# An eight-layer transformer on one core: later projections, transposes inside expert blocks, other score banks, and ternary weights prepared in an earlier stage

## The reference

```python
def act_quant(x):
    scale = 127.0 / jnp.clip(jnp.max(jnp.abs(x), axis=-1, keepdims=True), 1e-05)
    return jnp.clip(jnp.round(x * scale), -128, 127) / scale
def weight_quant(w):
    scale = 1.0 / jnp.clip(jnp.mean(jnp.abs(w)), 1e-05)
    return jnp.clip(jnp.round(w * scale), -1, 1) / scale
def bit_linear(x, w):
    return jnp.einsum('bsd,hd->bsh', act_quant(x), weight_quant(w))
h = bit_linear(x, w1)                            # 256 -> 1024
h = depthwise_conv1d(h.transpose(0, 2, 1), conv_w, conv_b)   # 3 taps
return bit_linear(silu(h.transpose(0, 2, 1)), w2)             # 1024 -> 256
```

## Time and profile before

| | us |
|---|---|
| median of 3 runs | 3054.76 (3051.03 to 3055.73) |
| the profiled execution's own time | 3083.54 |
| its span | 3081.8, mean granted PE clock 0.928 |

### The profile page before, as it was taken

The page is one execution under the profiler, slowest core; times in us unless marked ns, Lnnn a source line. Parts: engine busy times, 40 slices in busy tenths (PEclk is TensorE's granted clock), DMA queues, the critical chain, the costliest instruction groups (busy, mean ns, idle before and its releaser), DMA issues. The chain is left out here.

```text
span 3081.8 us, 47764 instructions
## 1 busy us (share of the span) xinstructions
PE 2581.3 (84%) x15928; PEld 1781.0 (58%) x15928; DVE 1374.2 (45%) x4831; ACT 1121.8 (36%) x2609; POOL 824.1 (27%) x878
## 2 busy tenths in 40 slices
PE   6998859999938878979999999984999559999586
PEld 4776437777714434547766555663888436666344
DVE  6987502222133444336643333430111357777665
ACT  4554311111118970114444333331333126666321
POOL 3443030000042210007754344503000401212442
PEclk8999879999979998979999999997999769999798
DMA  4232362222022110034210000035777410000000
GB/s 134 84 116 78 146 204 85 84 86 74 14 95 78 60 42 24 0 93 144 111 45 7 11 6 6 1 123 195 293 285 289 140 34 11 10 8 6 28 7 18
DMA packets 69923, 252.33 MB, mean 82 GB/s; under 512 B 16395, under 2 KB 32040, under 8 KB 52264
## 3 DMA queue, kind: packets, MB, share of 16 engines
...
...
## 5 line engine op out<-in xcount | busy, mean ns | idle before, releaser
L2597 PE MATMUL L_ffne_up<-L_ffne_xT,L_ffne_wu 128*128 128x128 f32 (+1 forms) x2144 | 391.5, 340 | 33.2 <-DVE L_ffne_xT L2521 23.3
L2597 PEld LDWEIGHTS L_ffne_up<-L_ffne_xT,L_ffne_wu 128*128 128x128 f32 x2144 | 332.2, 194 | 92.9 <-ACT L_ffne_hT L2508 27.5
L1349 PEld LDWEIGHTS L_xattn_pt<-ident,L_xattn_p 112*125 112x125 f32 x1536 | 207.3, 189 | 183.4 <-issue 77.5
L1044 POOL TENSOR_SCALAR L_xattn_p<-L_xattn_p,L_xattn_rec 112x375 f32<-112x375 f32 x256 | 311.6, 1225 | 0.0
L1349 PE MATMUL L_xattn_pt<-ident,L_xattn_p 112*125 112x112 f32 x1536 | 257.7, 289 | 20.9 <-DVE L_xattn_pt L1203 16.0
L1203 DVE COPY L_xattn_pt<-L_xattn_pt 125x336 f32<-125x336 f32 x448 | 216.9, 499 | 125.6 <-PE L_xattn_pt L1349 125.5
L2583 PE MATMUL L_ffne_dn<-L_ffne_wd,L_ffne_hT 128*112 128x256 f32 (+1 forms) x1200 | 266.2, 379 | 1.5 <-issue 1.5
L1186 DVE TENSOR_REDUCE L_xattn_least<-L_xattn_s 112x1 f32<-112x375 f32 x256 | 128.4, 543 | 250.7 <-PE L_xattn_s L1337 250.5
L2583 PEld LDWEIGHTS L_ffne_dn<-L_ffne_wd,L_ffne_hT 128*112 128x112 f32 (+1 forms) x1200 | 216.9, 183 | 39.7 <-issue 2.1
...
L1127 ACT ACTIVATE L_xattn_p<-L_xattn_ssb,L_xattn_least 112x375 f32<-112x375 f32 x256 | 153.8, 602 | 129.9 <-DVE L_xattn_least L1192 129.0
L1127 ACT ACTIVATE L_xattn_p<-L_xattn_s,L_xattn_least 112x375 f32<-112x375 f32 x256 | 145.1, 569 | 140.7 <-DVE L_xattn_least L1186 140.6
...
## 6 DMA issues: line engine op xcount, KB each, us to landing
...
```

Of the source, the lines that this page charges most:

```text
L1044: p = pool.tensor_scalar(p_sb[:, head % RP, :], p_sb[:, head % RP, :], rec[:, h, head:head + 1], None, ALU.mult)
L1349: m = pe.transpose(pt_ps[head % 2][0:KP, 0, kt * S:(kt + 1) * S], p_sb[:, head % RP, kt * KP:(kt + 1) * KP], ident[0:S, 0:S])
L2597: m = pe.matmul(up_ps[s % RING][k][:, 0, 0:RH], wu[:, h, c, k * FF + f * 128:k * FF + (f + 1) * 128], xT[:, h, c, q * RH:(q + 1) * RH], st ...
```

## The change

Six of the twelve stages are touched.

- Tanh attention: the projection of a batch and its residual come one batch later, the projection between the second and the third chunk of scores. PE's and DVE's loops are written out for all 16 batches.
- Both expert stages: the transposes of the next block's rows, and the copies, are placed after given up-steps (after steps 6, 8, 10, 12, 14, or after step 4) and no longer at the block's end.
- Wide attention: the four free banks are three for scores and one for jobs up to turn 6, and two and two from turn 7 on; the jobs have other slots there; transposes of a pair stand together ahead of the jobs, and both jobs ahead of the products. The narrow attention keeps its order and banks.
- Second routing stage: the ternary layer's weights are loaded here, ahead of the fills, and DVE makes the ternary weights (q1, q2), the 24 taps and a bf16 identity behind the slots. PE sums the weight sums ahead of the last four hosted projections. These tiles are kept until the end.
- Ternary layer: no weights are prepared; DVE normalises and spreads the first four batches; POOL normalises from the fifth on.

```diff
-                    if not isinstance(b, int) or b < NB - 1:
+                    if b < NB - 1:
...
-                    if not isinstance(b, int) or b > 0:
-                        ch = Chain(dve, chain, (b - 1) * PER)
+                    ch = Chain(dve, chain, max(0, (b - 2) * PER + 1))
+                    if b > 1:
+                        residual(b - 2, h, ch)
+                    if b > 0:
                         take_o(b - 1, 1 - h)
                         divide(b - 1, ch)
-                        residual(b - 1, 1 - h, ch)
...
-                each_batch(dve, body)
-                ch = Chain(dve, chain, (NB - 1) * PER)
+                for b in range(NB):
+                    body(b, b % 2)
+                ch = Chain(dve, chain, (NB - 2) * PER + 1)
+                residual(NB - 2, 0, ch)
                 take_o(NB - 1, 1)
...
                         transpose_x(b + 1, 1 - h)
+                    if b > 1:
+                        project(b - 2)
                     scores(b, h, 2)
...
-                    if not first:
-                        project(b - 1)
...
-                each_batch(pe, body)
+                for b in range(NB):
+                    body(b, b % 2)
+                project(NB - 2)
...
-        slots = [[K[0]], [K[1]], [K[2]], [K[3]], [K[4]], [K[5]], [K[6]], [K[7]], [Q[0]], [Q[1], V[0]],
-                 [Y], [V[1], V[2]], [V[3]], [V[4]], [V[5]], [X]]
+        slots = [[K[0]], [K[1]], [K[2]], [K[3]], [K[4]], [K[5], K[6]], [K[7]], [], [Q[0]], [Q[1]], [Y],
+                 [V[0]], [V[1], V[2]], [V[3]], [V[4], V[5]], [X]]
+        slots_loaded = [[], [], [], [], [], [], [], [], [Q[0]], [Q[1]], [Y], [], [], [], [], [X]]
...
-    NS, NJ = (3, 1) if wide else (4, 1)
...
+    FREE = 4 if wide else 5
+    SWITCH = FROM - 1 if wide else NB
...
+    def score_banks(b):
+
+        return 2 if wide and b >= SWITCH else FREE - 1
...
+        def jobs_at(b, head):
+
+            return (slots_loaded if wide and b < SWITCH else slots)[head]
+
         def slot_jobs(run, b, h, head, kinds):
-            for kind, i in slots[head]:
+            for kind, i in (jobs_at(b, head) if wide else slots[head]):
...
+            first = 2 if wide and turn >= SWITCH else FREE - 1
+            spare = range(first, FREE)
+            at = spare[planned[first] % len(spare)]
+            planned[first] += 1
+            bank_of[kind, i, b] = at
+            if at in last_user:
+                bank_free[kind, i, b] = last_user[at]
+            elif at < FREE - 1:
+                bank_free[kind, i, b] = ("score", SWITCH * H - 1, 0)
+            last_user[at] = (kind, b, i)
...
+        def wait_bank(pe, kind, i, b):
+
+            if (kind, i, b) in bank_free:
+                was, of, n = bank_free[kind, i, b]
+                if was == "score":
+                    pe.wait_ge(exp_done, of + 1)
+                else:
+                    pe.wait_ge(done[was], made(was, of, n))
...
-                    after(pe, exp_done if wide else low_done, b * H + pair + 2 - NS)
+                    after(pe, exp_done if wide else low_done, b * H + pair + 2 - score_banks(b))
...
                         scores(b, h, pair)
+                        together = wide and b >= SWITCH
                         trail(b, h, pair, LT, turn_p)
+                        if together:
+                            trail(b, h, pair + 1, LT, turn_p)
                         slot_jobs(job, b, h, pair, "kqvxyz")
-                        trail(b, h, pair + 1, LT, turn_p)
+                        if together:
+                            slot_jobs(job, b, h, pair + 1, "kqvxyz")
+                        else:
+                            trail(b, h, pair + 1, LT, turn_p)
                         if (pair - LP) % SIDE == 0:
                             trail(b, h, pair, LP, products)
-                        slot_jobs(job, b, h, pair + 1, "kqvxyz")
+                        if not together:
+                            slot_jobs(job, b, h, pair + 1, "kqvxyz")
...
+class TernaryWeights:
...
+    def begin(self, sp, ins):
+        for to, src in ((self.w1[:, :], ins["L3_ffn_w1"]), (self.w2[:, :], ins["L3_ffn_w2"]),
+                        (self.cw[:, :, :], ins["L3_ffn_conv_w"]), (self.cb[:, :], ins["L3_ffn_conv_b"])):
+            sp.dma_start(to, src).then_inc(self.w_in, 16)
...
+    def sum(self, pe, bank):
+        pe.wait_ge(self.ones_done, 1)
+        pe.wait_ge(self.wsum_done, 1)
+        pe.matmul(bank[:, 0, 0:2], self.ones[:, :], self.wsum[:, :], start=True, stop=True).then_inc(self.wsum_out, 1)
+
+    def prepare(self, dve, bank):
+
+        c = Chain(dve, self.chain)
+        c.step(dve.tensor_copy(self.identb[:, :], self.core.ident[:, :]))
+        dve.wait_ge(self.w_in, 64)
+        for n, w in enumerate((self.w1, self.w2)):
+            r = dve.tensor_reduce(self.wsum[:, n:n + 1], w[:, :], AX.X, ALU.add, apply_absolute_value=True)
+        r.then_inc(self.wsum_done, 1)
+        dve.wait_ge(self.wsum_out, 1)
+        c.link(dve.tensor_scalar(self.wmean[:, :], bank[:, 0, 0:2], 1.0 / (D * FF), EPS, ALU.mult, ALU.max))
+        c.link(dve.reciprocal(self.wscale[:, :], self.wmean[:, :]))
+        c.step(dve.tensor_scalar(self.cws[:, :, :], self.cw[:, :, :], self.wmean[:, 0:1], None, ALU.mult))
+        for n, (w, q) in enumerate(((self.w1, self.q1), (self.w2, self.q2))):
+            c.link(dve.tensor_scalar(w[:, :], w[:, :], self.wscale[:, n:n + 1], 1.0, ALU.mult, ALU.min))
+            c.link(dve.tensor_scalar(w[:, :], w[:, :], -1.0, self.MAGIC, ALU.max, ALU.add))
+            c.step(dve.tensor_scalar(q[:, :, :].rearrange("p a b -> p (a b)"), w[:, :], self.MAGIC, None, ALU.subtract))
+        for f in range(FC):
+            for j in range(3):
+                c.step(dve.tensor_scalar(self.taps[:, f, j, :], self.core.ident[:, :], self.cws[:, f, j:j + 1], None, ALU.mult))
+        dve.wait_ge(c.sem, c.n)
...
             def _(sp):
-                for to, src in ((w1[:, :], ins["L3_ffn_w1"]), (cw[:, :, :], ins["L3_ffn_conv_w"]),
-                                (cb[:, :], ins["L3_ffn_conv_b"]), (w2[:, :], ins["L3_ffn_w2"])):
-                    sp.dma_start(to, src).then_inc(w_in, 16)
...
-                for b in range(GB):
-                    normalize(b)
-                for b in range(GB):
-                    spread(b)
+                pool.wait_ge(xn_done, GB)
                 for b in range(GB, 2 * GB):
                     normalize(b)
-                pool.wait_ge(w_in, 64)
-                pool.wait_ge(wmean_done, 1)
-                ch.link(pool.tensor_scalar(w2[:, :], w2[:, :], wscale[:, 1:2], 1.0, ALU.mult, ALU.min))
-                ch.link(pool.tensor_scalar(w2[:, :], w2[:, :], -1.0, MAGIC, ALU.max, ALU.add))
-                pool.tensor_scalar(q2[:, :, :].rearrange("p a b -> p (a b)"), w2[:, :], MAGIC, None,
-                                   ALU.subtract).then_inc(q2_done, 1)
...
-                for f in range(FC):
-                    for j in range(3):
-                        r = act.activation(taps[:, f, j, :], ident[:, :], ACT.Copy, scale=cws[:, f, j:j + 1])
-                    r.then_inc(taps_done, 1)
-                    if f == 0:
-                        for b in range(GB):
-                            take_inverse(b)
+                for b in range(GB):
+                    take_inverse(b)
...
-                dve.wait_ge(w_in, 64)
-                for n, w in enumerate((w1, w2)):
-                    r = dve.tensor_reduce(wsum[:, n:n + 1], w[:, :], AX.X, ALU.add, apply_absolute_value=True)
-                r.then_inc(wsum_done, 1)
+                dve.wait_ge(rstd_done, 1)
+                for b in range(GB):
+                    dve.tensor_scalar(xn[:, b, :], x[:, b, :], core.mv[:, b, 0:1], core.rstd[:, b:b + 1],
+                                      ALU.subtract, ALU.mult).then_inc(xn_done, 1)
...
                 largest(0)
-                dve.wait_ge(identb_done, 1)
-                dve.wait_ge(wsum_out, 1)
-                c.link(dve.tensor_scalar(wmean[:, :], sc_ps[:, 0, 0:2], 1.0 / (D * FF), EPS, ALU.mult, ALU.max))
-                c.link(dve.reciprocal(wscale[:, :], wmean[:, :]))
-                dve.tensor_scalar(cws[:, :, :], cw[:, :, :], wmean[:, 0:1], None, ALU.mult).then_inc(wmean_done, 1)
-                c.link(dve.tensor_scalar(w1[:, :], w1[:, :], wscale[:, 0:1], 1.0, ALU.mult, ALU.min))
+                for b in range(GB):
+                    dve.tensor_scalar(invw[:, b, :], ones[0:S, :], amax[:, b:b + 1], None, ALU.mult).then_inc(invw_done, 1)
                 quantize(0)
-                c.link(dve.tensor_scalar(w1[:, :], w1[:, :], -1.0, MAGIC, ALU.max, ALU.add))
                 quantize(1)
-                dve.tensor_scalar(q1[:, :, :].rearrange("p a b -> p (a b)"), w1[:, :], MAGIC, None,
-                                  ALU.subtract).then_inc(q1_done, 1)
                 take_turned(0)
...
                 keys.begin(sp, ins)
+                if tw:
```

(20 more changed lines are left out.)

168 lines of the change are left out of this document (80 added, 88 removed).

## The result

The changed kernel takes 2952.87 us (median of 4 runs, 2949.59 to 2957.65) against 3052.9 of before (4 runs). The ratio is 0.9674 with a 95% interval of 0.9656 to 0.9692: 99.5 us off, where 61 were forecast and the range ended at 2967. Its profiled execution took 2949.59 us (span 2947.9, mean granted clock 0.934).

What follows compares the result with a forecast made beforehand. Each touched stage was taken to have its own limit: ACT and PE in tanh, PE in attentions and experts, POOL's puts in routing, waits in ternary. Terms -13 -10 -7 -20 +11 -23 = -62 gave 2993 us, range 2967 to 3021.

Steps and rivals of the forecast that it cites:

- Part 2: First expert stage, 8 blocks: PE's waits at the block's end go, 10 us off, bounds 7 and 11.
- part 4: Second expert stage, 35 blocks: the border wait for the xT copy goes, 20 us off, bounds 10 and 23.
- rival of late rows: Expert stages: next block's rows land after their mid-block use, making the kernel slower, up to 3097 us; chance 0.02.
- Part 3: Wide attention: job waits -12, exposed loads -5, score waits +8 and +2; sum -7, bounds +2 and -18.
- exposed loads: Wide attention: loads exposed between a K job and the scores are hidden by the new order, -5, possible 0 to 10.
- Part 1: Tanh attention: ACT's 0.98 us wait at each of 15 batch borders goes, 13 us off, bounds 5 and 15.
- The unrolled bodies: Tanh attention: writing out the loops was taken as 0, with 3 us either way left inside the bounds.
- Part 5: Second routing stage: 3.6 us from the delayed context load plus 7 from slowed puts, +11, bounds 0 and 18.
- Part 6: Ternary stage: opening 11.4 us earlier, group 0 stall and half-clock convolution gone; 23 us off, bounds 17 and 25.
- Pieces don't follow: Rival, whole kernel: tanh stays PE-bound, wide attention pays score waits, puts are starved; -32, 3023 us, chance 0.17.
- stall stays: Rival, ternary stage: POOL's normalises and spreads cause the slow DVE operations, 11.5 us stay; -50, 3005 us, chance 0.06.
- All goes: Rival, whole kernel: nothing blocks the puts and exposed weight loads go; -90, 2966 us, chance 0.12.

Runs made afterwards that it cites:

- only_exp: Kernel before with the expert hunks alone (transposes and copies after steps 6 to 14 or after step 4): 3006.05 us, ratio 0.9854.
- before_again: The kernel before, unchanged, profiled a second time: 3051.34 us, ratio 0.9999.
- tanh_unrolled: Kernel before with PE's and DVE's loops of the tanh attention written out for 16 batches, nothing else changed: 3046.52 us, ratio 0.9981.
- after_third: The changed kernel, unaltered, run again beside the late-load versions on one chip: 2952.09 us, ratio to before 0.9676.
- only_tern: Kernel before with only the ternary weight preparation in the second routing stage and the new ternary opening: ratio 0.9942.
- tern_passes: Changed kernel with three POOL passes over a scratch tile put back at the old place in the ternary stage: 2991.5 us, ratio to before 0.9689.
- prep_split: Changed kernel with DVE's six passes in the second routing stage cut into eight pieces of 256 columns each: ratio to before 0.9661.
- weights_late: Changed kernel with the ternary weight loads issued behind the fills and the third context batch: ratio to before 0.965.

## Why the prediction was wrong

The mechanisms held, part by part; the sizes did not, and the range was too narrow for that.

**Part 2 and part 4, experts.** Both terms were priced by the waits of the profile, 10.3 us and 0.69 a block, with upper bounds from the same rows (11 and 23). The step that failed is that a removed wait is worth its row. It was worth some 0.26 us more: 0.94 x 34 = 32 by the periods (29 by the stage, which has slower first blocks), and in the first stage the period went from 50.86 to 48.5, 2.36, for three waits of 1.65 us together (0.24 each on top). There were seven such borders, 16.5 us; the other 3.2 of that stage's 19.7 are the two stretches at half clock (only_exp), which the forecast had at nothing. The earlier trace rows also lacks two of the seven last waits, which the list puts under "issue": with them the printed waits are 11.5 us and not 10.3. The rows to read were the starts, 2239.30 to 2240.37 in the trace of before. 18 of the 38 us that the forecast missed lie in these two stages. The Trainium skill, Perfetto Trace Analysis, "Summary: the profiler window per engine type", says of TensorE that the profile shows an estimated end and leaves out the semaphore's way. The 0.16 us between 0.22 and 0.38 agree with the first half of that. The rival of late rows did not come: landings were 4.0 us at the median and 11.5 once, PE waited for rows once behind the stage's first load, 2.4 us.

**Part 3, wide attention.** -12 for the job waits was -19, the same 0.26 on each of 24. +8 +2 for the score waits was +14. -5 for exposed loads was about -13, beyond its end of 10; that term is inferred. The sum of the three is -18, and the stage gave 16.7 beside before_again alone and 19.7 beside the mean of the old form. Two of the three errors had one cause.

**Part 1, tanh attention.** 16.4 measured, 1.4 over the upper bound. The failed step is the price of a border: one printed wait, 0.98 us, 15 times, less 2 for PE. By the starts, 14 borders of before_again add 16.6 us to 1.91 each, and they alternate (3.02, then 3.35 us at 1044.35 to 1047.70 in the trace of before, where I read one border). All of it went. "The unrolled bodies: I take 0" failed too: they were worth 6.8 by themselves, and the move on top of them 9.6, where I had 13. That the sum of the two came near is luck; only tanh_unrolled shows it.

**Part 5, routing.** +11 against +8 to +10. The queue: third context load 5.1 us later, PE's first use of it 3.6 later (28.84 against 25.23 us from the stage's start), as worked out, but the first put 5.1 later: I let PE's slack of 1.4 us stand for the whole chain, and behind 4.0 us of idle time of PE the granted clock was 0.5 for 3.4 us (from 1966.9), so that PE's next products took 2.84 us in place of 1.51. In four other profiles with the early loads (after_third, only_tern, tern_passes, prep_split) the clock stayed at 0.5 for 6.8 us, and the first put came at 69.7 to 70.6 us and not at 68.3. Without them (weights_late) there was no such stretch. The puts: 3.9 lost and not 7. The direction from the spreads of POOL was right and its share (83%) too high, 3.9 of 7.5 us is 52%; the taps cost 0, where I had taken 1. The Trainium skill, SBUF - State Buffer, "SBUF: two separate sides", has such a transfer blocked until the end of DVE's operation and some 115 ns more. The three held puts agree: they end 0.12 us behind the end of a pass, but of the second pass that they meet. The Trainium skill's example there goes from 620 to 3100 ns beside a tensor_copy. Here a put went from 0.94 to 2.15 to 2.39 us, 2.3 to 2.5 times, and the rule taken as "all of it is lost" gave 13 us where 3.9 were measured. PE's first use of the third context load:

```profile
1967.22 2.84 PE L2043 MATMUL L_xattnkvr_ps<-L_xattnkvr_ctxT,L_xattnkvr_wk 128*128 128x375 f32 x4 [4.00 <-issue]
```

**Part 6, ternary.** Opening 12.6 for 11.4 (from rstd to the first up-product 10.5 us, 23.1 before), the stall and the convolution at half clock 12.4 for 11.5, 1.8 elsewhere. Each was near its term; the stage ended 2 us beyond the bound of 25.

**Rivals and range.** "Pieces don't follow" and "stall stays" are refuted. "All goes" (2966, 0.12) was the nearest, and 13 us short. The range took six costs as independent and got 17 us either way. All six were off to the same side, and the 0.26 us per wait is in three of them: a common error of a method is not reduced by having many terms. Even its favourable ends together gave only -90; the 0.26 us on 34 + 21 + 24 removed waits are another 20, against 21 score waits added.
